# Spreading each output-projection tile over four slots, two tiles a unit, and writing the batches out instead of looping

## The chip, the cores and the metric

The kernel runs on one core of one Trainium2 chip. The metric is the device time of one execution in microseconds (us); lower is better. Engines are called as in the profile: PE (TensorE, with its weight loads as PEld), DVE (VectorE), ACT (ScalarE), POOL (GpSimd) and SP, which only issues DMAs here. DVE, ACT, POOL and PE each run their own instructions in order and wait for each other through semaphores.

## What is computed

One transformer layer on x of shape (8, 1024, 512): causal attention with 16 heads of 32, its output projection, a layer norm and a residual, then a feed-forward part of width 2048 with a sine inside, again with layer norm and residual.

```python
def _L0_attn_ref(h, Wqvk, Wo):
    b, s, d = h.shape
    qvk = (h @ Wqvk).reshape(b, s, 3, H, HD)
    q, v, k = (qvk[:, :, 0], qvk[:, :, 1], qvk[:, :, 2])
    scores = jnp.einsum('bshi,bthi->bsth', q, k) + mask[None, :, :, None]
    weights = jax.nn.softmax(scores / math.sqrt(d), axis=2)
    wv = jnp.einsum('bsth,bthi->bshi', weights, v).reshape(b, s, d)
    return wv @ Wo
...
x = x + _layernorm(_L0_attn_ref(_layernorm(x), Wqvk, Wo))
x = x + _layernorm(_L0_ffn_ref(_layernorm(x), W1, b1, phases, w_real, w_imag, W2, b2))
```

## The kernel before

There are three phases one after the other: the projections to q, v and k, the attention, and the feed-forward part. The change touches the attention alone. Attention works through 8 batches. A batch is 4 **units** of 4 heads each, and a unit is 20 **slots** (`NS`): a slot is one block of 256 queries against 128 keys for the four heads, in the order of `STEPS`. A loop over slots is written out in Python for every engine, and each engine's program goes through the same slots (`for u, k in stage.slots`), so that a slot number names the same step on all of them.

What stands in slot k of a unit:

- PE: the scores of slot k (`scores`, into `a_pst`, two banks, so it waits until ACT has taken slot k-2), in two parts of two heads; the weighing of V with the probabilities of the slot six earlier (`weigh`, `LAG` = 6, into `a_acc`), in two parts; and between them shared items: **pieces** (score blocks of the next unit into `a_pw`, from which DVE takes row maxima), the turning of a maximum, and the turning of attended rows. A piece goes into one of two banks, and waits until DVE has released the piece two before it.
- ACT: the exponential of slot k (`a_prob`), then the float16 high half of the slot before (`a_prob_hi`), which is done for two slots at a time where the table allows it.
- POOL: the low half, `a_prob_lo = a_prob - a_prob_hi`, which `weigh` waits for.
- DVE: maxima of the pieces (`u_mx`), normalising (`a_rden`, `a_o`), and copying the turned rows into `a_oT`.

The **output projection** takes the attended rows of a batch, held turned in `a_oT`, and multiplies them by Wo: 8 tiles of 128 rows a batch, each tile 4 groups (`g`) of 3 matmuls of 128x512 into one bank (`a_pwo`). A tile belongs to the batch before, and is fitted into the slots of the units that follow. `WO_AT` gives the slot at which each tile starts, counted from the start of the batch's fourth unit: 10, 18, ..., 66. That puts the tiles at slots 10 and 18 of the fourth unit, 6 and 14 of the next batch's first, 2, 10 and 18 of its second and 6 of its third. Groups 0 and 1 stand at the very end of the tile's first slot and 2 and 3 at the end of the second. DVE then takes the tile's row statistics (`wo_stats`) two slots after its start, a reciprocal square root in eight small steps, and writes the result (`wo_out`) six slots after, which frees the bank.

```python
WO_AT = list(range(10, 10 + 8 * QT, 8))
WO_STATS, WO_OUT, WO_STORE = 2, 6, 7
...
                    for part in range(2):
                        for b, t in stage.tiles(u, k, part):
                            for g in range(2 * part, 2 * part + 2):
                                project(i, before, b, t, g, stage, parity)
```

The first batch (`FIRST`), the last (`LAST`) and what is left after it (`DRAIN`) are written out; the six between them run as a hardware loop of three rounds with two batches a round (`run_all`), in which the counts that instructions wait for are worked out in registers. The tiles of the last batch have a table of their own, `WO_AT_LAST`.

Of the kernel before, what the change touches and what calls it, by code (L numbers as in the profile page):

```python
# [23 lines left out]
F16 = mybir.dt.float16  # L24
# [5 lines left out]
P = 128  # L30
BATCH, SEQ, D = 8, 1024, 512
# [12 lines left out]
GROUPS = HEADS // HPG  # L44
# [110 lines left out]

WO_AT = list(range(10, 10 + 8 * QT, 8))


WO_AT_LAST = [10, 15, 20, 21, 25, 26, 28, 29]
OWN_BANK = {3: 0, 4: 1, 5: 2, 6: 3}  # L160
WO_STATS, WO_OUT, WO_STORE = 2, 6, 7
LAST_OUT, LAST_STORE = 3, 4
ROOT_STEPS = 8
ROOT_AT = {(2, 1): (0,), (3, 0): (1,), (3, 1): (2,), (4, 0): (3,), (4, 1): (4,), (5, 0): (5,), (5, 1): (6,), (6, 0): (7,)}

ROOT_BITS, ROOT_NEAR, ROOT_GAIN = 0x5F1FFFF9, 2.38924456, 0.703952253

assert all(TURN_AT[t // TQ] < at < 2 * NS + TURN_AT[t // TQ] for t, at in enumerate(WO_AT))
TAIL = WO_AT_LAST[-1] + LAST_STORE + 1 - NS
# [894 lines left out]
def attention_phase(nc, x, weights, units, feed, qk_parts, v_parts, x1, b2):  # L1064
# [11 lines left out]
    with ctx:  # L1076
        def sb(name, shape, dt=F32):
            return ctx.enter_context(nc.sbuf_tensor("a_" + name, shape, dt))
# [15 lines left out]
        o = sb("o", [P, 2, TQ, P])  # L1094
        oT = sb("oT", [P, 2, GROUPS + 1, SEQ], F16)
        stats = sb("stats", [P, YR, 6])
# [44 lines left out]

        FIRST_ON_POOL = QT * (BATCH - 1) + min(t for t, at in enumerate(WO_AT_LAST) if at + WO_STATS >= NS)

# [18 lines left out]
        def turned_group(g, batch_parity):  # L1162
            return GROUPS if g == 0 and batch_parity else g

        def run_all(engine, run):

            run(0, FIRST, 0)
            with engine.Fori(0, BATCH // 2 - 1) as pair:
                run(2 * pair + 1, MIDDLE, 1)
                run(2 * pair + 2, MIDDLE, 0)  # L1170
            run(BATCH - 1, LAST, 1)
            run(BATCH, DRAIN, 0)

        def sync(sp):
# [41 lines left out]

            run_all(sp, run)

        def tensor(pe):
# [126 lines left out]
            run_all(pe, run)  # L1346

        def scalar(act):
# [37 lines left out]
            act.wait_ge(const, CONST)  # L1386
            run_all(act, run)

        def vector(dve):
# [76 lines left out]
            def roots(i, stage, u, k, late):  # L1466

                for (lag, end), steps in ROOT_AT.items():
                    for b, t in stage.tiles(u, k, lag):
                        if end == late and not stage.last_batch(b):  # L1470
                            for step in steps:
                                wo_root(i + b, t, step)

# [38 lines left out]

            run_all(dve, run)

        def gpsimd(pool):
# [18 lines left out]
            def run(i, stage, parity):  # L1534
                for u, k in stage.slots:
# [491 lines left out]
```

## Time and profile before

| what | us |
|---|---|
| median of the runs (range) | 3295.58 (3291.59 to 3298.58) |
| the profiled execution: its time, its span | 3292.4, 3290.4 |
| projections to q, v, k, up to about | 564 |
| attention: first and last exponential | 564.2 to 1896.3 |
| busy over the span: PE, DVE, ACT, POOL | 3143.2, 2316.0, 2062.5, 1284.6 |

The profile is of one execution. Busy time of PE counts overlapping matmuls and says little about how much room is left; the starts of its instructions say more. In the attention phase the start of an exponential on ACT marks the slot, so the distance between the first exponentials of two units is the length of a unit, and four of them make a batch.

### The profile page before, as it was taken

Reading aid. Unit: us, or ns where it says so; the run is one execution under the profiler, and the core shown is the slowest. Engines: PE = TensorE matmul, PEld = TensorE weight load, DVE = VectorE, ACT = ScalarE, POOL = GpSimd, SP = SyncE. Lnnn points to the kernel's source line nnn. Section 1 sums busy time; section 2 is a strip of 40 time slices with the busy share of each in tenths; the row PEclk is TensorE's granted clock in tenths of the full one; section 3 lists DMA queues with packets and bytes.
Section 4 is the critical chain, followed back from the end, with each engine's and each line's share of the span. In section 5 each row is a group of like instructions: output and inputs, shape, how many; then the busy total and the mean of one; then the engine's idle time right before and its main releaser. Section 6 shows DMA issues by size and latency. Waiting matters only on the chain.

```text
span 3290.4 us, 77730 instructions
## 1 busy us (share of the span) xinstructions
PE 3143.2 (96%) x30020; PEld 1825.9 (55%) x30020; DVE 2316.0 (70%) x4747; ACT 2062.5 (63%) x2453; POOL 1284.6 (39%) x586
## 2 busy tenths in 40 slices
PE   7999999999998999899999899999999999999998
PEld 3444444776666676666676644444444444444443
DVE  5655556888887888788888756666666666666665
ACT  2223333998988898889898944554555454545453
POOL 1000000998988898989898910000000000000000
PEclk9999999999999999999999999999999999999999
DMA  4564853122222222222222230000000000000000
GB/s 150 194 211 140 264 186 118 54 67 86 74 86 71 75 75 81 75 85 75 77 75 82 69 141 26 26 26 26 25 23 16 18 20 25 25 25 25 26 26 26
DMA packets 194241, 246.65 MB, mean 75 GB/s; under 512 B 16960, under 2 KB 135936, under 8 KB 191872
## 3 DMA queue, kind: packets, MB, share of 16 engines
q1 hardware_dynamic: 193920, 242.25, 23.5%
q8 instruction: 216, 3.54, 0.5%
q14 instruction: 105, 0.86, 0.1%
HBM read 148.87 MB, written 92.80 MB: 73 GB/s over the span
## 4 chain that ended last, share of the span: by engine, by line
PE 59%; POOL 24%; issue 11%; DVE 4%; ACT 1%; DMA 1%; POOLq 0%; SPq 0%; ACTq 0%; DVEq 0%
POOL a_prob_lo L1522 24%; PE f_py L1915 20%; PE f_ph L1892 20%; PE q_pm L903 14%; DVE u_mx L330 1%; PE f_ph L1877 1%; PE q_pt L893 1%; PE a_acc L1307 1%; ACT a_prob_hi L1363 1%; PE a_pwo L1260 1%; PE a_pst L1278 0%; PE a_pw L311 0%; DMA qk_parts<-q_stage 0%; DVE s_work L234 0%; DVE q_amax L792 0%
## 5 line engine op out<-in xcount | busy, mean ns | idle before, releaser
L1522 POOL TENSOR_TENSOR a_prob_lo<-a_prob,a_prob_hi 128x2048 f16<-128x2048 f32 (+2 forms) x448 | 1191.7, 2694 | 146.0 <-ACT a_prob_hi L1363 145.0
L330 DVE TENSOR_REDUCE u_mx<-a_pw 128x1 f32<-128x512 f32 x1184 | 731.7, 656 | 179.2 <-PE a_pw L316 116.7
L1353 ACT ACTIVATE a_prob<-a_pst,a_lift,w_exp_scale 128x1024 f32<-128x1024 f32 (+1 forms) x640 | 707.2, 1122 | 133.5 <-PE a_pst L1278 92.5
L1915 PE MATMUL f_py<-f_w,f_act 128*128 128x512 f16 x3048 | 699.4, 379 | 1.3 <-DMA f_w<-w_parts 1.3
L1363 ACT ACTIVATE a_prob_hi<-a_prob 128x2048 f16<-128x2048 f32 (+2 forms) x448 | 583.3, 1302 | 0.0
L1849 ACT ACTIVATE f_hidden_work<-f_ph,w_turn,w_fold 128x512 f32<-128x512 f32 x256 | 199.2, 778 | 598.3 <-PE f_ph L1892 597.7
L1307 PEld LDWEIGHTS a_acc<-u_vt,a_prob_hi 128*128 128x128 f16 x9216 | 422.7, 96 | 130.4 <-POOL a_prob_lo L1522 39.4
L1307 PE MATMUL a_acc<-u_vt,a_prob_hi 128*128 128x33 f16 x9216 | 448.6, 178 | 45.3 <-POOL a_prob_lo L1522 34.9
L1278 PE MATMUL a_pst<-u_qp,u_kp 98*128 98x256 f16 (+1 forms) x2560 | 462.0, 262 | 30.8 <-ACT a_prob L1353 14.9
L241 POOL TENSOR_TENSOR s_ve<-s_mv,s_eps 128x4 f32<-128x4 f32 x31 | 8.9, 286 | 1235.9 <-DVE s_mv L227 1235.9
L1915 PEld LDWEIGHTS f_py<-f_w,f_act 128*128 128x128 f16 x3048 | 297.7, 98 | 348.5 <-DVE f_act L1757 2.6
L311 PE MATMUL a_pw<-u_kp,u_qp 96*128 96x512 f16 x1494 | 440.0, 328 | 34.9 <-DVE u_mx L330 28.5
L1307 PE MATMUL a_acc<-u_vt,a_prob_lo 128*128 128x33 f16 x4608 | 426.3, 177 | 0.0
L1771 DVE TENSOR_SCALAR f_hidden_work<-f_hidden_work 128x512 f32<-128x512 f32 x256 | 108.2, 423 | 392.5 <-ACT f_hidden_work L1849 390.6
L1307 PEld LDWEIGHTS a_acc<-u_vt,a_prob_lo 128*128 128x128 f16 x4608 | 363.3, 96 | 0.0
L903 PE MATMUL q_pm<-q_xT,q_w 128*128 128x512 f16 x1536 | 344.2, 381 | 2.6 <-DVE q_w L817 2.6
L1892 PE MATMUL f_ph<-f_xT,f_w 128*128 128x512 f16 x1152 | 264.3, 379 | 0.0
L1892 PE MATMUL f_ph<-s_xT,f_w 128*128 128x512 f16 x1152 | 264.3, 379 | 0.0
L1278 PEld LDWEIGHTS a_pst<-u_qp,u_kp 98*128 98x128 f16 x2560 | 194.4, 97 | 116.8 <-ACT a_prob L1353 22.4
L903 PEld LDWEIGHTS q_pm<-q_xT,q_w 128*128 128x128 f16 x1536 | 150.4, 98 | 177.5 <-issue 6.4
L843 ACT ACTIVATE q_stage<-q_pm 128x512 f16<-128x512 f32 x128 | 76.3, 597 | 243.9 <-PE q_pm L903 215.7
L1757 DVE TENSOR_TENSOR f_act<-f_hidden_work,f_act 128x512 f16<-128x512 f32 x256 | 177.1, 692 | 39.3 <-ACT f_act L1839 39.3
(197 smaller groups left out, 4043.4 us busy)
## 6 DMA issues: line engine op xcount, KB each, us to landing
qk_parts<-q_stage SPq DMA_DIRECT2D x128, 256.0 KB, 3.4
u_qp<-qk_parts SPq DMA_DIRECT2D x192, 128.0 KB, 2.6
u_kp<-qk_parts SPq DMA_DIRECT2D x192, 128.0 KB, 2.7
v_parts<-q_vstage SPq DMA_DIRECT2D x16, 1056.0 KB, 5.3
u_vt<-v_parts SPq DMA_DIRECT2D x32, 528.0 KB, 4.5
q_x<-in_L_attn_h_dram SPq DMA_DIRECT2D x16, 1024.0 KB, 10.2
q_raw<-in_L_ffn_W_dram SPq DMA_DIRECT2D x16, 1024.0 KB, 8.0
u_xr<-in_L_attn_h_dram SPq DMA_DIRECT2D x64, 256.0 KB, 3.0
```

Of the source, the lines that this page charges most:

```text
L311: last = pe.matmul(out[:, s * n:(s + 1) * n], units.qp[b][0:KQ, i // TPC, h, i % TPC * P:(i % TPC + 1) * P], units.kp[b][0:KQ, h, half_ * ...
L330: dve.tensor_reduce(out, src[:, 0:n * len(heads)].rearrange("p (h n) -> p h n", n=n), AX_X, ALU.max).then_inc(units.released, 1)
L903: return pe.matmul(pm[:, m % BANKS, :], lhs, rhs, **flags)
L1278: last = pe.matmul(pst[:, slot, h, off:QC], kp[b][:, h, j * P:(j + 1) * P], qp[b][:, c * QC // CH, h, c * QC % CH + off:c * QC % CH + QC], ...
L1307: last = pe.matmul(acc[:, (t * HPG + h) * VF:(t * HPG + h + 1) * VF], part[:, k % HR, h, t * P:(t + 1) * P], vt[:, b, j, col:col + VF], st ...
L1353: act.activation(prob[:, k % PR, :, off:QC], pst[:, k % 2, :, off:QC], ACT.Exp, scale=exp_scale, bias=lift[:, :]).then_inc(exp_done, 1)
L1363: act.activation(prob_hi[:, first % HR:first % HR + steps, :, off:QC], prob[:, first % PR:first % PR + steps, :, off:QC], ACT.Copy).then_i ...
L1522: pool.tensor_tensor(prob_lo[:, first % HR:first % HR + steps, :, off:QC], prob[:, first % PR:first % PR + steps, :, off:QC], prob_hi[:, f ...
L1757: dve.tensor_tensor(act_r[:, r, 1, :], arg[:, s, :], act_r[:, r, 0, :], ALU.subtract).then_inc(act_lo, 1)
L1849: act.activation(arg[:, s, :], ph[:, bank_of("hidden", f), :], ACT.Identity, bias=turn0[:, f:f + 1], scale=fold[:, 0:1]).then_inc(arg_done, 1)
L1892: last = pe.matmul(ph[:, bank_of("hidden", f), :], w1_of(a, k, f), xT_of(e, b, k), start=(j == 0), stop=(j == len(terms) - 1))
L1915: last = pe.matmul(py[:, t, :], act_r[:, f % AR, b, t * P:(t + 1) * P], w2_of(a, f), start=(f == 0 and j == 0), stop=(f == NF - 1 and j == ...
```

## The change

A tile now starts every 10 slots instead of every 8 (`WO_AT`), so that every unit has two, at slots 0 and 10, in the same places. It runs over four slots instead of two, one group of 3 matmuls in each, and the group stands ahead of the slot's weighing instead of at the slot's end. DVE's statistics, steps and output move with it: four and eight slots after the tile's start instead of two and six. The last tiles of a batch are read while the next batch's second unit is being turned, so `a_oT` holds groups 0 and 1 twice instead of group 0 alone. The last batch's own tiles keep their two slots and their delays (`LAST_PARTS`, `LAST_STATS`), but stand ahead of the weighings too. The loop over batches is gone: all eight batches are written out, with constants in place of registers.

```diff
-WO_AT = list(range(10, 10 + 8 * QT, 8))
+WO_AT = list(range(10, 10 + 10 * QT, 10))
...
-WO_STATS, WO_OUT, WO_STORE = 2, 6, 7
-LAST_OUT, LAST_STORE = 3, 4
+WO_STATS, WO_OUT, WO_STORE = GROUPS, GROUPS + 4, GROUPS + 5
+LAST_PARTS, LAST_STATS, LAST_OUT, LAST_STORE = 2, 2, 3, 4
...
-        oT = sb("oT", [P, 2, GROUPS + 1, SEQ], F16)
+        oT = sb("oT", [P, 2, GROUPS + 2, SEQ], F16)
...
-            return GROUPS if g == 0 and batch_parity else g
+            return GROUPS + g if g < 2 and batch_parity else g
...
-            with engine.Fori(0, BATCH // 2 - 1) as pair:
-                run(2 * pair + 1, MIDDLE, 1)
-                run(2 * pair + 2, MIDDLE, 0)
+            for i in range(1, BATCH - 1):
+                run(i, MIDDLE, i % 2)
...
+            def tiles_of_slot(i, u, k, before, stage, parity):
+
+                for part in range(GROUPS):
+                    for b, t in stage.tiles(u, k, part):
+                        parts = LAST_PARTS if stage.last_batch(b) else GROUPS
+                        for g in range(part * GROUPS // parts, (part + 1) * GROUPS // parts if part < parts else 0):
+                            project(i, before, b, t, g, stage, parity)
...
                         if part >= 2 and e:
                             weigh(i, *e, part - 2)
+                        if part == 1 and e and stage.this:
+                            tiles_of_slot(i, u, k, before, stage, parity)
...
-                    for part in range(2):
-                        for b, t in stage.tiles(u, k, part):
-                            for g in range(2 * part, 2 * part + 2):
-                                project(i, before, b, t, g, stage, parity)
+                    if not (e and stage.this):
+                        tiles_of_slot(i, u, k, before, stage, parity)
```

How the instructions move, in three places. First PE, in the second unit of a middle batch of the kernel before, slot 2 and the start of slot 3. `a_pst` are scores, `a_pw` pieces, `a_acc` the weighing (it goes on for 24 matmuls), `a_pwo` the tile.

```order
L1278 MATMUL a_pst<-u_qp,u_kp 128x256 x2
L1061 REGISTER_ALU
L311 MATMUL a_pw<-u_kp,u_qp 128x512
L316 MATMUL a_pw<-u_mask_q,u_identb 128x128
L1296 REGISTER_ALU
L1307 MATMUL a_acc<-u_vt,a_prob_hi 128x33 x2
...
L1307 MATMUL a_acc<-u_vt,a_prob_lo 128x33
L1061 REGISTER_ALU
L1260 MATMUL a_pwo<-w_wo,a_oT 128x512 x6
L1061 REGISTER_ALU
L1278 MATMUL a_pst<-u_qp,u_kp 128x256 x2
```

The same slot 2 of a unit in the kernel after. Slots 0, 1 and 3, and 10 to 13, have the same shape:

```order
L1276 MATMUL a_pst<-u_qp,u_kp 128x256 x2
L1258 MATMUL a_pwo<-w_wo,a_oT 128x512 x3
L311 MATMUL a_pw<-u_kp,u_qp 128x512
L316 MATMUL a_pw<-u_mask_q,u_identb 128x128
L1305 MATMUL a_acc<-u_vt,a_prob_hi 128x33 x2
```

Six matmuls at the end of the slot became three between the slot's second scores and its weighing; the other three are in slots 0, 1 and 3.

Second, PE at the end of the loop's body in the kernel before, from the last turning of slot 19:

```order
L1241 MATMUL a_pw<-u_ident,a_o 128x128 x2
...
L1307 MATMUL a_acc<-u_vt,a_prob_lo 128x33
L1260 MATMUL a_pwo<-w_wo,a_oT 128x512 x6
L1168 REGISTER_ALU
L1168 COMPARE_AND_BRANCH
```

In the kernel after, PE has no branch anywhere in the attention phase; the next unit's scores follow.

Third, DVE in the kernel after, in slots 13 to 15 (`a_stats` are a tile's statistics, `a_root` the steps of its root, `u_mx` the maxima of pieces):

```order
L330 TENSOR_REDUCE u_mx<-a_pw 128x2
L1418 CAST a_oT<-a_pw 128x256
L1420 TENSOR_TENSOR a_oT<-a_pw,a_oT 128x256
L1426 BN_STATS a_stats<-a_pwo 128x6
L1428 COPY a_seen<-a_stats 128x1
L1429 BN_AGGR a_mv<-a_stats 128x2
L330 TENSOR_REDUCE u_mx<-a_pw 128x2
L330 TENSOR_REDUCE u_mx<-a_pw 128x1 x2
L1439 TENSOR_SCALAR a_root<-a_mv,w_wo_eps 128x1
L1443 TENSOR_SCALAR a_root<-a_root 128x1
L330 TENSOR_REDUCE u_mx<-a_pw 128x1 x2
```

In the kernel before, the statistics of a tile at slot 10 stood ahead of slot 12's maxima; now they stand ahead of slot 14's three.

## Rows read from the trace of the kernel before

**Rows 1.** Stretches: first batch's fourth unit; three units of the fourth, of the last.

```profile
core 0: us, PE busy (x) PEld busy (x) DVE busy (x) ACT busy (x) POOL busy (x), PEclk, DMA share, GB/s
675.65:716.09 40.44, 37.38 (x630) 28.21 (x628) 31.70 (x72) 37.45 (x36) 37.74 (x15) 1.00 0.23 67
1054.94:1181.94 127.00, 118.32 (x2007) 88.58 (x2006) 106.53 (x260) 112.75 (x102) 108.36 (x42) 1.00 0.28 80
1729.00:1856.60 127.60, 118.08 (x2007) 88.68 (x2006) 106.38 (x261) 112.86 (x102) 111.05 (x43) 1.00 0.30 89
```

**Rows 2.** Stretches: a unit without tiles, and one with three.

```profile
600.70:638.10 37.40, 34.17 (x636) 27.07 (x635) 29.92 (x59) 37.03 (x35) 37.16 (x15) 1.00 0.21 60
1097.82:1141.20 43.38, 40.41 (x640) 29.32 (x638) 34.10 (x85) 37.61 (x35) 37.69 (x15) 1.00 0.30 85
```

**Rows 3.** Stretches: the first and the last of the six middle batches.

```profile
716.10:884.20 168.10, 155.92 (x2633) 116.64 (x2632) 138.34 (x333) 150.40 (x136) 148.97 (x57) 1.00 0.27 78
1561.40:1729.00 167.60, 155.88 (x2635) 116.80 (x2633) 138.63 (x335) 150.25 (x136) 148.98 (x57) 1.00 0.28 79
```

**Rows 4.** Waits, 714 to 1856 us: who waited for whom, total, times, longest.

```profile
ACT a_prob L1353 <- PE a_pst L1278: 88.1, 102, 1.6
ACT a_prob L1353 <- PE a_pst L1283: 37.0, 52, 3.4
```

**Rows 5.** ACT in time, unit without tiles: slots 0, 3, 4, 13 with 14.

```profile
600.77 1.22 ACT L1353 ACTIVATE a_prob<-a_pst,a_lift,w_exp_scale 128x1024 f32<-128x1024 f32 x1
...
605.60 1.23 ACT L1353 ACTIVATE a_prob<-a_pst,a_lift,w_exp_scale 128x1024 f32<-128x1024 f32 x1
607.07 1.21 ACT L1353 ACTIVATE a_prob<-a_pst,a_lift,w_exp_scale 128x1024 f32<-128x1024 f32 x1 [0.23 <-PE a_pst L1283]
...
624.37 2.57 ACT L1353 ACTIVATE a_prob<-a_pst,a_lift,w_exp_scale 128x1024 f32<-128x1024 f32 x2
```

**Rows 6.** ACT in time, unit 1097.82: exponentials of slots 4, 9 with 10, 14.

```profile
1106.59 1.21 ACT L1353 ACTIVATE a_prob<-a_pst,a_lift,w_exp_scale 128x1024 f32<-128x1024 f32 x1 [1.80 <-PE a_pst L1283]
...
1116.69 2.31 ACT L1353 ACTIVATE a_prob<-a_pst,a_lift,w_exp_scale 128x1024 f32<-128x1024 f32 x2
...
1128.12 1.20 ACT L1353 ACTIVATE a_prob<-a_pst,a_lift,w_exp_scale 128x1024 f32<-128x1024 f32 x1 [0.39 <-PE a_pst L1278]
```

**Rows 7.** PE in time: first scores of slots 0 and 4, unit 1054.94.

```profile
1053.85 0.39 PE L1278 MATMUL a_pst<-u_qp,u_kp 98*128 98x256 f16 x2 [2.62 <-issue]
...
1060.38 0.38 PE L1278 MATMUL a_pst<-u_qp,u_kp 98*128 98x256 f16 x2
```

**Rows 8.** PE in time, unit without tiles: slots 0, 10, a weighing, slot 14.

```profile
597.96 0.38 PE L1278 MATMUL a_pst<-u_qp,u_kp 98*128 98x256 f16 x2
...
616.70 0.38 PE L1278 MATMUL a_pst<-u_qp,u_kp 98*128 98x256 f16 x2
...
621.62 0.20 PE L1307 MATMUL a_acc<-u_vt,a_prob_hi 128*128 128x33 f16 x2 [0.27 <-POOL a_prob_lo L1522]
...
624.71 0.38 PE L1278 MATMUL a_pst<-u_qp,u_kp 98*128 98x256 f16 x2
```

**Rows 9.** PE in time, unit 1097.82: half a tile, slot 10, a piece, slot 14.

```profile
1104.09 1.46 PE L1260 MATMUL a_pwo<-w_wo,a_oT 128*128 128x512 f16 x6
...
1116.44 0.38 PE L1278 MATMUL a_pst<-u_qp,u_kp 98*128 98x256 f16 x2
...
1124.56 0.39 PE L311 MATMUL a_pw<-u_kp,u_qp 96*128 96x512 f16 x1 [0.47 <-DVE u_mx L330]
...
1127.15 0.38 PE L1278 MATMUL a_pst<-u_qp,u_kp 98*128 98x256 f16 x2
```

**Rows 10.** The loop's line on PE's sequencer; ACT behind and without the branch.

```profile
L1168 PEldq COMPARE_BRANCH  x3: 83/3959/4078, 1049.6 to 1726.4; - x3
1393.54 1.20 ACT L1353 ACTIVATE a_prob<-a_pst,a_lift,w_exp_scale 128x1024 f32<-128x1024 f32 x1 [3.38 <-PE a_pst L1283]
1222.63 1.20 ACT L1353 ACTIVATE a_prob<-a_pst,a_lift,w_exp_scale 128x1024 f32<-128x1024 f32 x1 [0.49 <-PE a_pst L1283]
```

More of the change, by code:

```diff
@@ L150 @@
 K_FREE_AT = max(k for k, (_c, j) in enumerate(STEPS) if j < TPC) + 1
-WO_AT = list(range(10, 10 + 8 * QT, 8))
+WO_AT = list(range(10, 10 + 10 * QT, 10))
 WO_AT_LAST = [10, 15, 20, 21, 25, 26, 28, 29]
 OWN_BANK = {3: 0, 4: 1, 5: 2, 6: 3}
-WO_STATS, WO_OUT, WO_STORE = 2, 6, 7
-LAST_OUT, LAST_STORE = 3, 4
+WO_STATS, WO_OUT, WO_STORE = GROUPS, GROUPS + 4, GROUPS + 5
+LAST_PARTS, LAST_STATS, LAST_OUT, LAST_STORE = 2, 2, 3, 4
 ROOT_STEPS = 8
-ROOT_AT = {(2, 1): (0,), (3, 0): (1,), (3, 1): (2,), (4, 0): (3,), (4, 1): (4,), (5, 0): (5,), (5, 1): (6,), (6, 0): (7,)}
+ROOT_AT = {(WO_STATS + (n + 1) // 2, (n + 1) % 2): n for n in range(ROOT_STEPS)}
 ROOT_BITS, ROOT_NEAR, ROOT_GAIN = 0x5F1FFFF9, 2.38924456, 0.703952253
-assert all(TURN_AT[t // TQ] < at < 2 * NS + TURN_AT[t // TQ] for t, at in enumerate(WO_AT))
+assert all(TURN_AT[t // TQ] < at < 3 * NS + TURN_AT[t // TQ] for t, at in enumerate(WO_AT))
 TAIL = WO_AT_LAST[-1] + LAST_STORE + 1 - NS
@@ L1139, in attention_phase @@
         BANKS_LEFT = 6
-        FIRST_ON_POOL = QT * (BATCH - 1) + min(t for t, at in enumerate(WO_AT_LAST) if at + WO_STATS >= NS)
+        FIRST_ON_POOL = QT * (BATCH - 1) + min(t for t, at in enumerate(WO_AT_LAST) if at + LAST_STATS >= NS)
         def on_pool(n):
@@ L1162, in turned_group, with run_all @@
         def turned_group(g, batch_parity):
-            return GROUPS if g == 0 and batch_parity else g
-        def run_all(engine, run):
+            return GROUPS + g if g < 2 and batch_parity else g
+        def run_all(run):
             run(0, FIRST, 0)
-            with engine.Fori(0, BATCH // 2 - 1) as pair:
-                run(2 * pair + 1, MIDDLE, 1)
-                run(2 * pair + 2, MIDDLE, 0)
+            for i in range(1, BATCH - 1):
+                run(i, MIDDLE, i % 2)
             run(BATCH - 1, LAST, 1)
@@ L1215, in run @@
                             store_max(sp, units, unit % 2, half)
-            run_all(sp, run)
+            run_all(run)
         def tensor(pe):
@@ L1340, in run @@
                         last.then_inc(feed.tr_done, 1)
-                    for part in range(2):
-                        for b, t in stage.tiles(u, k, part):
-                            for g in range(2 * part, 2 * part + 2):
-                                project(i, before, b, t, g, stage, parity)
-            run_all(pe, run)
+                    if not (e and stage.this):
+                        tiles_of_slot(i, u, k, before, stage, parity)
+            run_all(run)
         def scalar(act):
@@ L1386, in scalar @@
             act.wait_ge(const, CONST)
-            run_all(act, run)
+            run_all(run)
         def vector(dve):
@@ L1466, in roots @@
             def roots(i, stage, u, k, late):
-                for (lag, end), steps in ROOT_AT.items():
+                for (lag, end), step in ROOT_AT.items():
                     for b, t in stage.tiles(u, k, lag):
                         if end == late and not stage.last_batch(b):
-                            for step in steps:
-                                wo_root(i + b, t, step)
+                            wo_root(i + b, t, step)
             def shared(i, at, before, what, unit, m, stage, parity):
@@ L1484, in run @@
                     for b, t in stage.tiles(u, k, WO_STATS):
+                        if not stage.last_batch(b):
+                            wo_stats(i + b, t, stage)
+                    for b, t in stage.tiles(u, k, LAST_STATS):
+                        if not stage.last_batch(b):
+                            continue
                         wo_stats(i + b, t, stage)
-                        if stage.last_batch(b) and stage is not DRAIN:
+                        if stage is not DRAIN:
                             for step in range(ROOT_STEPS):
@@ L1511, in run @@
                         scale_rows(dve, feed, 0, 1, feed.work, feed.xin[:, 0], feed.normed)
-            run_all(dve, run)
+            run_all(run)
         def gpsimd(pool):
@@ L1540, in run @@
                         deviations(pool, feed, 0, 1)
-                    for b, t in stage.tiles(u, k, WO_STATS):
+                    for b, t in stage.tiles(u, k, LAST_STATS):
                         if stage is DRAIN:
@@ L1552, in gpsimd @@
             pool.wait_ge(units.v_stored, 16 * NCH + START)
-            run_all(pool, run)
+            run_all(run)
         turned_last = (released, work_before(BATCH, DRAIN) + len(DRAIN.work))
```

## The prediction

> **What bounds the kernel now.** The change acts in the attention alone, 1332 us of the profiled execution's 3292.4. I first cut the trace into stretches that end at the first exponential of a unit, and compared units with and without tiles. The first batch's second unit has none and lasts 37.40 us, a unit with three lasts 43.38 [rows 2]; the busy columns, in the order of the heading in [rows 1], give ACT 37.0 and 37.6, POOL 37.2 and 37.7. So ACT and POOL are full in the unit without tiles, and what the tiles add, ACT spends idle. The waits say for whom: ACT waited for scores 88.1 + 37.0 us between 714 and 1856 [rows 4]. The six middle batches take 1729.0 - 716.1 = 1012.9 us [rows 3], 42.2 a unit.
>
> A tile is 12 matmuls of 128x512. Six of them take 1.46 us with the last one's own tail of about 0.38, so one starts every 0.215 [rows 9], a group of three costs PE 0.65 and a tile 2.58. The question is how much of it PE can take without making ACT late.
>
> Two quantities settle it. The first is ACT's pace with nothing to wait for: in slots 0 to 3 the exponentials start 4.83 us apart from slot 0 to slot 3 and the fourth needs 1.09 (605.60 to 607.07 is 1.47, of which 0.38 is late scores) [rows 5]: 5.92. In slots 10 to 13 it is 7.2: slot 13's exponential and the next take 2.57 together [rows 5] where two at full pace take 2.31 [rows 6], so that unit loses 0.27 there. ACT's floor for a unit is 37.40 - 0.38 - 0.27 = 36.8. The second is PE's lead: the time from the first score of a slot to its exponential. It is 600.77 - 597.96 = 2.81 at slot 0 [rows 5, 8] and about 1.0 to 1.2 when ACT only just has to wait (at slot 4 the scores follow the tile at 1104.09 + 6 x 0.215 = 1105.38, and 1106.59 - 1105.38 = 1.21; at slot 14 1128.12 - 1127.15 = 0.97) [rows 6, 9].
>
> **The tile at slots 0 to 3.** Without a tile PE needs 1060.38 - 1053.85 = 6.53 us for these four slots when nothing holds it [rows 7]. With four groups it is 6.53 + 2.58 = 9.11. It starts 2.81 ahead, so slot 4's scores begin 6.30 after slot 0's exponential, and slot 4's exponential follows at 6.30 + 1.21 = 7.51, against the floor of 5.92: **1.6 us** late. Today's tile at slots 2 and 3 makes the same exponential 1106.59 - 1097.82 = 8.77 after the start [rows 2, 6], 2.9 late: there PE first idles in slots 0 to 2 for the low halves and then works the whole tile in a row. The new groups stand ahead of the weighing, where that wait is, and fill it. Bounds: 1.2, should the lead at slot 0 grow by 0.4, and 2.9.
>
> **The tile at slots 10 to 13.** The unit without tiles goes from slot 10 to slot 14 in 624.71 - 616.70 = 8.01 on PE [rows 8]. Adding up the starts that are further apart than such matmuls otherwise are, 1.15 of it are waits: 0.45 for a low half in front of slot 12's weighing (the row shows 0.27 of it as idle), the rest small ones for the banks of the pieces. That leaves 6.86, with a tile 9.44. Unit 1097.82, whose tile starts at slot 10 in the old way, needs 1127.15 - 1116.44 = 10.71 [rows 9]. I take 9.6: the low half is there 0.65 later for nothing, and DVE, which in these slots has nine maxima at some 0.63, a normalising, a turning and a maximum to split, about 8 us when no statistics fall into them, keeps up with a PE that needs 9.4. The lead at slot 10 is 1116.69 + 1.09 - 1116.44 = 1.34 [rows 6, 9]. Slot 14's exponential is then at -1.34 + 9.6 + 1.0 = 9.3 after slot 10's, **2.1 us** over 7.2. Bounds: 1.9 (no waits left) and 1128.12 - 1117.78 - 7.2 = 3.1, what the tile costs now.
>
> **What moves on DVE** I cost at nothing. Statistics at slot 4 fall where PE has 1.9 us of work and ACT 2.9. At slot 14 they delay three maxima by about 1 us; ACT's slot is again 2.9 long, and PE has 3.3 us of work in slots 14 and 15 against 4.0 of ACT, so with a lead of 1.0 it can lose about 0.7 to 1 before ACT sees it. If that cover is gone it costs up to 0.5 a unit. DVE's present wait for a tile, as its statistics come right behind it, ends: two slots lie between now. The bank is free two slots after `wo_out` as before. The first tile of a batch, at slot 10 of the fourth unit, now comes sooner after the turning of slot 9 that it needs: 0 to 0.5 in one unit of four. The second copy of group 1 in `a_oT` adds no instruction.
>
> **A unit** thus takes 36.8 + 1.6 + 2.1 = 40.5 us. POOL needs 37.7 [rows 2], 2.8 less. Six batches: 24 x 40.5 = 972.0.
>
> **The loop.** PE's branch takes 3959 and 4078 ns the two times it is taken, 83 the third [rows 10]; behind a taken one ACT idles 3.38 us for scores, at the same place without a branch 0.49 [rows 10], so a jump costs 2.9 and two 5.8. The Trainium skill bears on this: "Runtime: NRT & Kernel Launch", Instruction fetch mechanics, says that a taken branch whose target is not in the fetched window stops execution until it is fetched, and the trace agrees with its 3.96 and 4.08 us. "Advanced Engine Details and Errata", Control Flow Timing, gives about 108 ns for a compare-and-branch; the sum by that would be an estimate of 0.2 us in place of 5.8, and the row decides against it. The register instructions that vanish cost nothing now: the last batch, written out with constants already, is no faster in its first three units than the fourth, 127.60 and 127.00 us [rows 1].
>
> **The sum**, against the profiled 3292.4:
> - two jumps: -5.8
> - the other units of the six middle batches: 972.0 - (1012.9 - 5.8) = -35.1
> - the last batch's first three units, 127.6 now [rows 1], 121.5 then: -6.1
> - the first batch's fourth unit has one tile instead of two, 40.4 [rows 1] to 36.8 + 0.4 + 2.1 = 39.3: -1.1
> - the last batch's fourth unit gets a tile at slot 0 that it did not have; at most 1.6, but POOL bounds that unit: +1.0
>
> Together -47.1, so 3245.3 for the profiled execution; it lies 3.2 under the median of 3295.58, so the median becomes **3248**. A measurement here tells about 0.2% (6.6 us) from no change.
>
> **The rivals.**
> 1. *DVE's waits remain* (0.14). The piece at 1124.56 waited 0.47 for DVE [rows 9], right behind a tile's statistics. If the pieces of slots 12 to 15 go on waiting, because DVE carries two tiles in each unit where it now has one to three, the second tile keeps its 3.1 and slot 14 adds 0.5: 36.8 + 1.6 + 3.1 + 0.5 = 42.0 a unit. 27 units (24 + 3) are then 1134 against 1140.5 with their jumps, and the kernel ends at about 3289. Half of it gives 41.25 and 3269. For it: DVE is busy 34.1 us of 43.4 with three tiles and 29.9 of 37.4 with none [rows 2], and not evenly. Against: the statistics left the crowded slot 12.
> 2. *Spreading does nothing, two tiles a unit cost their full price* (0.07), the case on the slower side. PE has no wait left in slots 0 to 3 of unit 1053.85 [rows 7], and a PE that is late stays late, in four slots as in two. Then each unit pays 2.9 + 3.1: 42.8, 27 units 1155.6, that is 15 more than now: about 3311. It decides from 42.24 a unit on. Against: the lead of 2.81 at slot 0, which today's tiles at slots 2, 6 and 10 hardly use.
> 3. *More is hidden* (0.09): the lead at slot 0 grows, slots 10 to 13 lose all waits, and the following slots carry some of it: 39.7 a unit or less, 3226 or below.
> 4. *The written-out program pays in fetching what the jumps cost* (0.04). The last batch is written out already, and its first three units take 127.60 where the fourth batch's take 127.00 [rows 1]: 0.6 a batch, six times 3.6 of the 5.8, 3252, inside the range.
>
> **How the numbers follow.** The forecast, 39.9 to 41.5 a unit, has 0.66, and rival 4 lies within it with 0.04. Its own bounds (27 x 0.6 = 16 down, 27 x 1.0 = 27 up) give 3232 to 3275; the range reaches a little into rivals 1 and 3: **3228 to 3276**. Faster by over 0.2%: 0.66 + 0.04 + 0.09 and 0.11 of rival 1; within 0.2%: 0.04, the far end of rival 1 and the near end of 2; slower: 0.06.
>
> **What the profile will show.** Units all alike near 40.5 us, and batches near 162. PE's first scores of slot 4 some 6.3 after slot 0's exponential. No wait for a low half in front of the weighings of slots 0, 2 and 12. ACT's wait for scores in attention down from 125 to about 100 us. No idle of 3 us at 1051 and 1389. I am wrong if units differ by place as now, if pieces wait for DVE in slots 14 and 15 with ACT idle behind them, or if slot 0's lead is well below 2.8.

## The result, and the profile after

| kernel | median us (range, executions) | ratio to before | 95% interval |
|---|---|---|---|
| before | 3295.01 (3291.59 to 3298.58, 4) | | |
| after | 3254.27 (3253.64 to 3255.36, 4) | 0.9877 | 0.9859 to 0.9894 |

The median falls by 40.7 us; the forecast was 3248, 6 us too low. The profiled execution of the kernel after took 3255.4 us, with a span of 3253.6, where the sum said 3245.3: 10 too low. The difference is that the forecast added 3.2 for the distance of a profiled execution from the median, and this one lies 1.1 above its own. Attention, from first to last exponential, went from 1332.1 to 1295.6 us (563.2 to 1858.8).

First the stretches of the kernel after: a unit of the first middle batch, that whole batch, three units of the third middle batch and of the last batch, and the last unit. They answer to [rows 1 to 3].

```profile
core 0: us, PE busy (x) PEld busy (x) DVE busy (x) ACT busy (x) POOL busy (x), PEclk, DMA share, GB/s
714.69:755.29 40.60, 38.24 (x659) 29.38 (x658) 35.10 (x83) 37.27 (x35) 37.17 (x15) 1.00 0.31 82
714.69:877.46 162.77, 153.26 (x2634) 117.58 (x2633) 140.40 (x332) 149.12 (x137) 148.70 (x57) 1.00 0.30 82
1040.42:1162.20 121.78, 114.36 (x1971) 87.85 (x1970) 105.24 (x249) 111.53 (x103) 111.09 (x43) 1.00 0.28 80
1692.14:1813.94 121.80, 114.75 (x1975) 88.14 (x1974) 105.29 (x249) 111.84 (x103) 111.49 (x43) 1.00 0.25 73
...
1813.94:1858.79 44.85, 32.51 (x544) 24.36 (x543) 31.68 (x72) 36.15 (x33) 41.80 (x17) 0.84 0.24 80
```

Units no longer differ by place: 40.6 us for the first three of each batch, 40.9 for the fourth, and a batch 162.8 instead of 168.1 and 167.6. ACT and POOL are busy as long as before; what went is ACT's idle time. Only the last unit is worse, 44.85 against 39.7 before.

Next the waits from 714 to 1856 us: who waited for whom, total us, times, longest. They answer to [rows 4].

```profile
PEld a_acc L1305 <- POOL a_prob_lo L1532: 45.8, 84, 1.1
...
ACT a_prob L1359 <- PE a_pst L1276: 41.8, 64, 1.5
ACT a_prob L1359 <- PE a_pst L1281: 32.3, 29, 1.4
...
PEld a_pw L311 <- DVE u_mx L330: 28.4, 56, 0.7
...
PE a_pw L311 <- DVE u_mx L330: 15.1, 28, 0.6
```

ACT's wait for scores is 74.1 us; it was 125.1 [rows 4]. A further 19.8 us of such waits (19 times) is booked as for POOL. In the unit below that happens at slot 14, 1.03 us behind PE's first scores of that slot (1108.49), which is the lead that the forecast gave an exponential that only just waits for scores. So I count them as scores too: 93.9, near the forecast's 100. What came last there, POOL or PE, the runs don't take apart.

Now ACT in time, unit 1081.38, exponentials of slots 0, 3, 4, 13 and 14 (answers to [rows 6]):

```profile
1081.38 1.22 ACT L1359 ACTIVATE a_prob<-a_pst,a_lift,w_exp_scale 128x1024 f32<-128x1024 f32 x1
...
1086.58 1.21 ACT L1359 ACTIVATE a_prob<-a_pst,a_lift,w_exp_scale 128x1024 f32<-128x1024 f32 x1 [0.23 <-PE a_pst L1276]
1088.93 1.20 ACT L1359 ACTIVATE a_prob<-a_pst,a_lift,w_exp_scale 128x1024 f32<-128x1024 f32 x1 [1.15 <-PE a_pst L1281]
...
1107.28 1.21 ACT L1359 ACTIVATE a_prob<-a_pst,a_lift,w_exp_scale 128x1024 f32<-128x1024 f32 x1 [0.91 <-PE a_pst L1276]
1109.52 1.20 ACT L1359 ACTIVATE a_prob<-a_pst,a_lift,w_exp_scale 128x1024 f32<-128x1024 f32 x1 [1.03 <-POOL a_prob_lo L1532]
```

And PE there: the first scores of slots 0, 4 and 10, and the first group of the tile (answers to [rows 7, 9]):

```profile
1078.57 0.38 PE L1276 MATMUL a_pst<-u_qp,u_kp 98*128 98x256 f16 x2
...
1079.45 0.81 PE L1258 MATMUL a_pwo<-w_wo,a_oT 128*128 128x512 f16 x3
...
1087.68 0.38 PE L1276 MATMUL a_pst<-u_qp,u_kp 98*128 98x256 f16 x2
...
1098.68 0.38 PE L1276 MATMUL a_pst<-u_qp,u_kp 98*128 98x256 f16 x2
```

PE is 1081.38 - 1078.57 = 2.81 ahead at slot 0, needs 1087.68 - 1078.57 = 9.11 for the four slots and brings slot 4's scores 6.30 after slot 0's exponential: the three numbers of the forecast to the hundredth. Slot 4's exponential is 7.55 behind slot 0's, 1.63 over the 5.92 of ACT's pace. In slots 10 to 13 PE takes 1108.49 - 1098.68 = 9.81, a little more than the 9.6 of the forecast, with a lead of 1.44 instead of 1.34 and 1.03 left at slot 14: slot 14's exponential comes 9.40 behind slot 10's, 2.2 over the pace of 7.2. In this unit PE waits for low halves at slots 8 and 18 only, in front of none of the weighings of slots 0, 2 and 12.

### The profile page after: what moved, and what is told of

Read it like the earlier page. It is cut to its first block, busy times and chain, and to the rows that moved or that the text cites. A ratio compares the mean times of both kernels' runs of the same rounds, so it can differ in the third digit from the quotient of the medians.

```text
span 3253.6 us, 72496 instructions
## 1 busy us (share of the span) xinstructions
PE 3124.1 (96%) x30020; PEld 1831.8 (56%) x30020; DVE 2331.3 (72%) x4747; ACT 2054.9 (63%) x2453; POOL 1283.4 (39%) x586
## 4 chain that ended last, share of the span: by engine, by line
PE 80%; DVE 9%; POOL 5%; ACT 3%; issue 2%; DMA 1%; SPq 0%; ACTq 0%; POOLq 0%
PE f_py L1925 20%; PE f_ph L1902 20%; PE q_pm L903 15%; PE a_acc L1305 6%; PE a_pst L1276 5%; PE a_pw L311 5%; POOL a_prob_lo L1532 4%; PE a_pwo L1258 4%; DVE u_mx L330 4%; ACT a_prob_hi L1369 2%; PE a_pst L1281 1%; ACT a_prob L1359 1%; PE a_pw L316 1%; PE f_ph L1887 1%; PE q_pt L893 1%
## 5 line engine op out<-in xcount | busy, mean ns | idle before, releaser
L330 DVE TENSOR_REDUCE u_mx<-a_pw 128x1 f32<-128x512 f32 x1184 | 745.3, 657 | 143.4 <-PE a_pw L316 83.7
L1276 PE MATMUL a_pst<-u_qp,u_kp 98*128 98x256 f16 (+1 forms) x2560 | 461.8, 262 | 30.2 <-ACT a_prob L1359 27.5
L1305 PE MATMUL a_acc<-u_vt,a_prob_hi 128*128 128x33 f16 x9216 | 448.1, 178 | 40.5 <-POOL a_prob_lo L1532 27.9
L1276 PEld LDWEIGHTS a_pst<-u_qp,u_kp 98*128 98x128 f16 x2560 | 187.2, 97 | 90.0 <-ACT a_prob L1359 35.7
```

The lines of the kernel that those rows point to most:

```text
L330: dve.tensor_reduce(out, src[:, 0:n * len(heads)].rearrange("p (h n) -> p h n", n=n), AX_X, ALU.max).then_inc(units.released, 1)
L1276: last = pe.matmul(pst[:, slot, h, off:QC], kp[b][:, h, j * P:(j + 1) * P], qp[b][:, c * QC // CH, h, c * QC % CH + off:c * QC % CH + QC], ...
L1305: last = pe.matmul(acc[:, (t * HPG + h) * VF:(t * HPG + h + 1) * VF], part[:, k % HR, h, t * P:(t + 1) * P], vt[:, b, j, col:col + VF], st ...
```

## The experiments

Their ratios are to the kernel before, on the same chip; its medians there were 3293.2 to 3293.7. "A unit" is the distance of the first exponentials of two units.

**The loop kept.** The kernel after, with the hardware loop and its registers put back.

```diff
-            for i in range(1, BATCH - 1):
-                run(i, MIDDLE, i % 2)
+            with engine.Fori(0, BATCH // 2 - 1) as pair:
+                run(2 * pair + 1, MIDDLE, 1)
+                run(2 * pair + 2, MIDDLE, 0)
```

> The kernel after with the six middle batches in the hardware loop again, all else as it is there. My theory: the two taken branches give back 2.9 us each and nothing else changes, 3254.3 + 5.8 = 3260; every unit stays 40.6 to 40.9 apart from the two behind a jump. Rival, the register instructions of the loop cost time too, now that TensorE is late in more slots: units longer by 0.1 or more everywhere, 3265 or above. Rival, the jump costs only its instruction, 0.1 us each: 3254.5.

3269.87 us, ratio 0.993 (0.9913 to 0.9946): 15.6 over the kernel after, more than twice what was expected. Its branch on PE, PE's first scores behind it and ACT's waits:

```profile
L1168 PEldq COMPARE_BRANCH  x3: 82/4613/4739, 1037.2 to 1705.5; - x3
...
1042.11 0.60 PE L1278 MATMUL a_pst<-u_qp,u_kp 98*128 98x256 f16 x2 [4.42 <-issue]
1043.79 1.48 PE L1260 MATMUL a_pwo<-w_wo,a_oT 128*128 128x512 f16 x3
...
1044.04 1.20 ACT L1361 ACTIVATE a_prob<-a_pst,a_lift,w_exp_scale 128x1024 f32<-128x1024 f32 x1 [3.56 <-PE a_pst L1283]
...
1047.81 0.78 ACT L1361 ACTIVATE a_prob<-a_pst,a_lift,w_exp_scale 128x512 f32<-128x512 f32 x1 [2.06 <-PE a_pst L1283]
```

The stretches before and behind the branch (columns as above), and behind that of the kernel before:

```profile
1028.00:1037.50 9.50, 8.41 (x175) 6.68 (x174) 9.19 (x25) 9.50 (x8) 7.03 (x3) 1.00 0.16 47
1037.50:1042.10 4.60, 0.19 (x8) 0.08 (x4) 0.62 (x2) 2.98 (x3) 4.60 (x2) 0.92 0.41 126
1042.10:1045.50 3.40, 3.39 (x14) 1.74 (x14) 0.69 (x1) 1.46 (x2) 3.08 (x2) 0.50 0.54 159
1045.50:1049.00 3.50, 3.50 (x48) 2.55 (x47) 1.38 (x2) 1.44 (x3) 1.16 (x1) 0.62 0.30 80
```

```profile
1050.90:1053.80 2.90, 0.33 (x2) 0.00 (x0) 0.23 (x1) 0.78 (x1) 2.90 (x1) 1.00 0.64 170
1053.80:1057.00 3.20, 3.15 (x63) 2.62 (x64) 3.00 (x9) 2.06 (x3) 2.85 (x3) 1.00 0.34 86
```

The jump takes 0.65 longer, and then three things come together. PE's lead at slot 0, which the new tile uses up, is gone. The granted clock is 0.50, the lower level (1.2 GHz), for 3.4 us, and 0.62 in the next 3.5; before, it stayed at 1.00. The tile's three matmuls take 1.48 instead of 0.81. The unit that ends with the jump takes 44.7 (44.8 at the second) and the one behind it 44.2 (44.3), in place of 40.9 and 40.6: 7.5 a jump by these rounded lengths, 14.4 for two against the very same units of the kernel after. A jump costs 2.9 us in the old order and over 7 in the new one. How that divides among the three, no run takes apart.

The other twenty units of the middle batches are together 3.3 us longer than in the kernel after, and the last batch's first three 1.1. In nearly all the longer ones PE waits for a small transfer (4 KB, into `u_qp`); the waits from 714 to 1856 us, here and in the kernel after:

```profile
PE a_pst L1278 <- DMA u_qp<-u_nm: 10.0, 14, 1.2
```

```profile
PE a_pst L1276 <- DMA u_qp<-u_nm: 1.8, 4, 0.7
```

Away from the jumps, middle units without such a wait are 40.6 to 40.7 long, as in the kernel after, so the registers, which stand in all of them, cost under 0.1 a unit. Only the third unit in each round is 40.9 without it, which stays open. The time alone, 3269.87, would not have told this from the rival on registers, which said 3265 or above. Attention is 18.0 us longer in this trace than in that of the kernel after, while the whole execution is 13.2 longer: the part behind attention is 4.4 shorter (1390.4 against 1394.8), and what makes it so is open.

**Written out alone.** The kernel before, with only that part of the diff (the one above, turned round).

> The kernel before with its batches written out and nothing else changed. My theory: two jumps of 2.9 us go, 3295 - 5.8 = 3289, and the written-out batches run as the fourth did, 42.9, 43.4, 40.7 and 40.9 us a unit. Rival, straight code pays in fetching: 0.6 a batch back, 3292 to 3293. Rival, the register instructions cost time: under 3285.

3289.14 us (10 executions), ratio 0.9989 (0.998 to 0.9999). The jumps are gone, and 4 of the expected 5.8 us show. Its units run as the loop's do or 0.05 to 0.1 shorter (42.80, 43.39 and 40.69 against 42.92, 43.40 and 40.74), so straight code costs nothing that shows here. Two places in its trace give some back: one unit of the fifth batch is 2.6 longer than its like, where PE waited for a small DMA, and the last unit takes 43.7 instead of 39.7. Both come up again below.

**Even places alone.** All of the kernel after but the four slots and the place ahead of the weighing.

```diff
-WO_STATS, WO_OUT, WO_STORE = GROUPS, GROUPS + 4, GROUPS + 5
+WO_STATS, WO_OUT, WO_STORE = 2, 6, 7
...
-                        parts = LAST_PARTS if stage.last_batch(b) else GROUPS
+                        parts = LAST_PARTS
...
-                        if part == 1 and e and stage.this:
-                            tiles_of_slot(i, u, k, before, stage, parity)
...
-                    if not (e and stage.this):
-                        tiles_of_slot(i, u, k, before, stage, parity)
+                    tiles_of_slot(i, u, k, before, stage, parity)
```

> The kernel after, but each tile again in two slots, its six matmuls at the end of each slot, and statistics and output two and six slots after the start as before. So this is the even placing alone, tiles at slots 0 and 10 of every unit. My theory: spreading and the place ahead of the weighing carry the gain; a tile at slots 0 and 1 costs 2.1 us and one at 10 and 11 its old 3.1: 36.8 + 2.1 + 3.1 = 42.0 a unit, 27 x 1.35 = 36 us more than after, about 3290. Rival, the even placing is what gains: within 5 us of 3254.

3291.43 us, ratio 0.9993 (0.9983 to 1.0002): nothing. Units take 41.9, the mean of the uneven ones. Two tiles a unit are worth nothing by themselves. Some units of its trace are longer, up to 44.2; in that one PE waits 1.73 us for the small transfer.

**Four slots, at the slot's end.** The kernel after with only the last two pieces of that diff.

> The kernel after with each tile over four slots, but its group of three matmuls at the end of the slot, behind the weighing. My theory: TensorE waits 0.5 us for the low half in slot 0 again, which the group no longer fills, and slot 4's exponential is that much later; in slot 12 the low half is there by then. 41.1 us a unit, 27 x 0.5 = 13 us more: 3268. Rival, only the number of slots matters: 3254, no wait for a low half in slot 0 or as many as are hidden elsewhere. Rival, both waits come back in full (slot 0 and slot 12): 3280.

3272.09 us, ratio 0.9935 (0.9919 to 0.9952), 41.3 a unit. Spreading brings 19 us over the last kernel and the place ahead of the weighing a further 18. Of the 19, the shorter units are 27 x 0.54 = 14.6; most of the rest are the single long units of the last kernel, which this trace doesn't have (PE waits 0.4 us for the small transfer, there 9.9). Why the place matters, from PE in time, the first weighing of a slot 0:

```profile
1085.49 0.22 PE L1305 MATMUL a_acc<-u_vt,a_prob_hi 128*128 128x33 f16 x2 [0.34 <-POOL a_prob_lo L1529]
```

PE stands idle for the low half and then does the group; in the kernel after the group fills that wait. PE waits 35.9 us (82 times) for low halves in this kernel and 21.8 (57) in the kernel after, once more a unit. Slot 4's exponential comes 8.08 behind slot 0's instead of 7.55: the 0.5 that was expected. The other 0.2 of the unit's 0.7 fall in slots 10 to 13 (9.60 instead of 9.40), where this trace shows no such wait; what they are is open.

**Later starts.** The kernel after with the tiles at slots 2 and 12 of a unit, and at 1 and 11. Shown is the first.

```diff
-WO_AT = list(range(10, 10 + 10 * QT, 10))
+WO_AT = list(range(12, 12 + 10 * QT, 10))
```

> The kernel after with every tile two slots later, at slots 2 to 5 and 12 to 15 of each unit; statistics and output move with it to slots 6 and 10, 16 and 20. My theory: what a tile costs is set by how much of TensorE's work falls into slots where ScalarE is slow (4 and 14 last 2.9 us for 1.9 and 1.8 us of matmuls), so the first tile costs 1.1 instead of 1.6 and the second 1.9 instead of 2.2: 39.8 a unit, 27 x 0.8 = 22 less, 3232. Rival, VectorE decides: its statistics now fall ahead of slots 6 to 10, which have two runs of three maxima, and pieces wait for it there; no gain, 3254 or more.

> The kernel after with every tile one slot later, at slots 1 to 4 and 11 to 14. By the same theory half of that gain: 40.2 a unit, 3243. By the rival about 3254, since statistics at slots 5 and 15 are as good as at 4 and 14.

3281.76 us (ratio 0.9965, 0.9951 to 0.9979) and 3281.96 (0.9964, 0.995 to 0.9978), 41.8 a unit both: the rival. At slots 2 to 5 PE's part went as hoped, 1.1 over ACT's pace in place of 1.6. But pieces wait for DVE, in the first of them:

```profile
PEld a_pw L311 <- DVE u_mx L330: 67.4, 162, 0.6
...
PE a_pw L311 <- DVE u_mx L330: 27.5, 81, 0.5
```

162 and 81 waits instead of 56 and 28, behind statistics and steps that now stand among the maxima of slots 6 to 10. In the unit at 1089.16 PE waits so at slots 7, 8 and 10, and what the unit loses there (slot 10's exponential 12.6 behind slot 4's instead of 11.2) is more than the 0.5 gained before.

**Statistics twice.** The kernel after with each tile's first statistics done twice, the first into a spare tile: 0.6 us more for DVE a tile, with nothing else changed.

```diff
+                dve.bn_stats(again[:, :], projected(t, stage))
                 dve.bn_stats(a_stats[:, :], projected(t, stage))
```

> The kernel after with each tile's row statistics (0.69 us) taken twice by VectorE, the first time into a tile that nobody reads. Slot 4 has room. At slot 14 a piece already waits 0.70 us for VectorE, and TensorE's lead at slot 16 is 1.04 us, as small as it gets, so ScalarE is only just not held up. My theory: the second statistics show up nearly in full there, 0.6 a unit, 27 x 0.6 = 16 more: 3270. Rival, VectorE has room to spare, as its share of busy time (about 85%) suggests: within 4 us of 3254.

3282.7 us, ratio 0.9966 (0.9952 to 0.998): 41.6 a unit, so 1.2 us of work on an engine that is busy 35 of 40.6 cost 1.0 us of time, where 0.6 was expected. PE in time, the third piece of slot 14, here and in the kernel after:

```profile
1119.87 0.39 PE L311 MATMUL a_pw<-u_kp,u_qp 96*128 96x512 f16 x1 [1.14 <-DVE u_mx L330]
```

```profile
1110.49 0.39 PE L311 MATMUL a_pw<-u_kp,u_qp 96*128 96x512 f16 x1 [0.55 <-DVE u_mx L330]
```

The kernel after waits 0.55 for DVE at this slot, and ACT's long slot hides it: slot 16's exponential comes 3.99 behind slot 14's, as in the kernel before. With 0.59 more of waiting it comes 4.51 behind: 0.5 of the 1.0, so there is no reserve. The other 0.45 are lost before slot 14 (28.59 into the unit instead of 28.14), where "slot 4 has room" was expected: a piece waits 0.42 for DVE 15.6 us into the unit, which in the kernel after none does.

**Roots on POOL.** In the kernel after, the eight steps of each root are taken from DVE and done by POOL in two instructions. DVE's busy time in a batch falls from 140.4 to 132.3 us by it, POOL's rises from 148.7 to 154.2.

```diff
-                            for step in range(ROOT_STEPS):
-                                wo_root(i + b, t, step)
...
+                    for b, t in stage.tiles(u, k, WO_STATS):
+                        if not stage.last_batch(b):
+                            last_tile_root(t, QT * (i + b) + t)
```

> The kernel after, with the eight-step root of every tile of the middle batches taken off DVE: POOL makes it in two instructions (add, power), as the last tiles have it already. DVE is freed of 8 small instructions a tile, some 1.5 us, and POOL gets about 0.75 us a tile. Theory (DVE stands exactly at its edge, PE is the bound at 40.6 us a unit): as PE's order is unchanged, little comes back; 40.2 to 40.6 a unit, 3244 to 3255 us. Rival (POOL, at 38 us of 40.6, makes low halves late when it gets 1.5 us more a unit): 41.0 a unit or more, 3265 us.

> The same roots on POOL, and the tiles at slots 2 and 12 of each unit. With the roots on DVE these places gave 41.8 us a unit, and the traces put it down to DVE, whose statistics delayed pieces, while PE at slots 2 to 5 lost only 1.1 in place of 1.6. Theory (that was DVE): with 3 us a unit fewer on DVE the waits for pieces shrink, and the unit goes to 39.8 to 40.6, 3232 to 3255 us. Rival A (it is the two statistics themselves, behind which three maxima queue, not the roots): 41.5 or more, 3274 us and above. Rival B (POOL is late instead): waits for low halves appear, 41.2 or more.

> The same roots on POOL, with the tiles at slots 1 and 11 of each unit. With roots on DVE these places gave 41.8 us a unit. Theory (DVE was the cause): 40.1 to 40.6 a unit, 3240 to 3255 us. Rival A (statistics, not roots): 41.5 or more, 3274 us and above. Rival B (POOL late): waits for low halves appear, 41.2 or more.

At the old places 3250.09 us (3249.26 to 3252.16), ratio 0.9872 (0.9855 to 0.9888), units 40.5: DVE's relief returns 0.1 a unit, and by the intervals the kernel is not told from the kernel after. Its second middle batch, for the load (POOL is the last column of busy time):

```profile
875.93:1038.42 162.49, 152.77 (x2634) 117.73 (x2633) 132.25 (x268) 149.31 (x137) 154.21 (x73) 1.00 0.28 81
```

At slots 2 and 12, 3264.01 us (0.9917, 0.99 to 0.9933), 41.1 a unit instead of 41.8; at 1 and 11, 3276.4 (0.9952, 0.9936 to 0.9969), 41.5 instead of 41.8. The waits of the first:

```profile
PEld a_pw L311 <- DVE u_mx L330: 39.4, 108, 0.5
...
PE a_pw L311 <- DVE u_mx L330: 6.8, 27, 0.3
```

The waits for DVE fell from 27.5 to 6.8 us on PE and the time with them, 17.8 us, so DVE was a cause of the loss at those places. It was not all of it: 41.1 lies between theory and both rivals, and 41.5 is where rival A began. The traces show rival B's sign as well, POOL late. PE in time at slot 0's weighing, in the first kernel and in the second:

```profile
1122.92 0.22 PE L1305 MATMUL a_acc<-u_vt,a_prob_hi 128*128 128x33 f16 x2 [0.61 <-POOL a_prob_lo L1527]
```

```profile
1128.65 0.21 PE L1305 MATMUL a_acc<-u_vt,a_prob_hi 128*128 128x33 f16 x2 [0.77 <-POOL a_prob_lo L1527]
```

With the roots on DVE this wait is 0.29 at either place, and no group of a tile stands in front of it at slots 1 or 2. Slot 4's exponential now comes 7.22 instead of 7.03 behind slot 0's in the first kernel, and 7.85 instead of 7.36 in the second. An estimate from this: POOL takes back 0.2 and 0.5 a unit, and DVE's relief by itself is worth 0.9 and 0.7. In all, PE waits 17.4 and 21.5 us for low halves instead of 7.7 and 7.9. What keeps the rest, with the roots gone from DVE, stays open.

**The last unit.** The scaling of the first rows of the feed-forward part (`scale_rows`, 4 instructions) moved from slot 14 to 17 of the last unit, behind the normalising.

```diff
-    FEED_LOAD, FEED_STATS, FEED_SCALE = 0, 6, 14
+    FEED_LOAD, FEED_STATS, FEED_SCALE = 0, 6, 17
```

> The kernel after with the four scalings of the feed-forward part's first rows moved in VectorE's order from the end of slot 14 of the very last unit to the end of slot 17, behind the normalising that TensorE waits for. In the kernel after they take 10.75 us beside GpSimd and TensorE then waits 8.4 us for that normalising; the last unit is 44.8 us. My theory: that wait goes, the last unit is near 39 us, and some of it comes back since the scaled rows are later: 3249. Rival, the rows are needed as soon as the last unit ends, so all of it comes back: 3254, or later.

3256.26 us, ratio 0.9885 (0.9869 to 0.9902), not faster. PE in time at the end of attention, in the kernel after and in this one:

```profile
1856.57 0.22 PE L1305 MATMUL a_acc<-u_vt,a_prob_hi 128*128 128x33 f16 x2 [8.39 <-DVE a_o L1411]
```

```profile
1850.68 0.20 PE L1305 MATMUL a_acc<-u_vt,a_prob_hi 128*128 128x33 f16 x2 [1.71 <-DVE a_o L1411]
...
1862.61 1.86 PE L1258 MATMUL a_pwo<-w_wo,a_oT 128*128 128x512 f16 x4 [8.70 <-DVE a_oT L1420]
```

The last unit shrinks from 44.8 to 37.9, and a wait as long stands one step later. The scaling itself takes long. Its line in the last unit of the kernel before, of the kernel written out alone, of the kernel after, with one of the feed-forward part and POOL's line beside it (ns, shortest, median, longest):

```profile
L234 DVE TENSOR_SCALAR s_work<-s_x,s_mv,s_rstd x4: 1372/1949/4303, 1881.1 to 1886.2; 128x512 f32<-128x512 f32 x4
```

```profile
L234 DVE TENSOR_SCALAR s_work<-s_x,s_mv,s_rstd x4: 1377/2994/4298, 1876.1 to 1883.3; 128x512 f32<-128x512 f32 x4
```

```profile
L234 DVE TENSOR_SCALAR s_work<-s_x,s_mv,s_rstd x4: 1024/2829/4308, 1842.2 to 1848.7; 128x512 f32<-128x512 f32 x4
...
L234 DVE TENSOR_SCALAR s_work<-s_x,s_mv,s_rstd x4: 540/543/544, 2016.3 to 2017.7; 128x512 f32<-128x512 f32 x4
...
L1532 POOL TENSOR_TENSOR a_prob_lo<-a_prob,a_prob_hi x4: 1346/4242/4265, 1842.9 to 1852.7; 128x2048 f16<-128x2048 f32 x3, 128x512 f16<-128x512 f32 x1
```

## Why the forecast came close, and where its sum was off

**The mechanism holds.** The four slots, and the group ahead of the weighing, did what the sum said: 9.11 us of PE with no wait, 1.63 late at slot 4 (forecast 1.6), 2.2 at slots 10 to 13 (2.1, where 0.2 more on PE and 0.1 more lead partly cancel). Rival 2 (spreading does nothing) is refuted by the ladder: written out 3289, even places 3291, four slots 3272, ahead of the weighing 3254. Taken in this order, nearly the whole gain is from these last two steps. Rival 3 did not come: slot 0's lead stayed 2.81. Rival 4, pay in fetching, is tested by the kernel written out alone, whose units are no longer than the loop's; in the kernel after all batches are straight code, so their equal lengths say nothing on it.

**Term by term.** The profile shows -36.5 in attention for the -47.1 of the sum.
- *Six batches and two jumps*, forecast 972.0: 1692.14 - 714.69 = 977.4, 5.4 more. A unit is 40.6 instead of 40.5, the fourth 40.9 (a wait for the turning of slot 9, forecast 0 to 0.5, is 0.3), and two or three units are 0.2 to 0.4 over their like.
- *The last batch's first three units*: 121.8, forecast 121.5.
- *The first batch's fourth unit*: 39.2, as forecast. But the batch ends 0.7 later than the sum has it, as its first unit, which the change doesn't touch, is 37.5 instead of 36.5.
- *The last unit*: forecast +1.0, measured +5.1. This term was off by 4.1 us, two fifths of the whole miss, and the one whose mechanism was wrong; the six batches are off by more in sum, but by half a per cent of their 972.

**The step that failed** is "at most 1.6, but POOL bounds that unit: +1.0". I looked at what the tile costs PE and at POOL's busy time, and not at DVE's scaling there. Up to slot 18 the unit is hardly longer than before (its exponential comes 35.0 us after slot 0's, before 34.7); what is new stands in front of slot 19's, 9.8 behind it instead of 5.0. ACT's wait there, before and after:

```profile
1896.29 0.78 ACT L1353 ACTIVATE a_prob<-a_pst,a_lift,w_exp_scale 128x512 f32<-128x512 f32 x1 [2.01 <-PE a_pst L1283]
```

```profile
1858.79 0.78 ACT L1359 ACTIVATE a_prob<-a_pst,a_lift,w_exp_scale 128x512 f32<-128x512 f32 x1 [6.83 <-PE a_pst L1281]
```

PE waits in front of it for DVE's `a_o`, 3.6 us before and 8.4 after. In DVE's order the scaling stands ahead of `a_o` and ends 3.0 before it in both. The scaling takes 9.34 us in the kernel before (from 1881.13 on) and 10.75 after (from 1842.23), where its like take 0.54 each. Each of the four ends about 0.3 behind one subtraction of POOL: that from 1844.23 takes 4.27, and the scaling from 1844.47 takes 4.31. Before, one of the four sat out the whole of a 128x2048 subtraction, after, two did.

The larger part is that DVE comes to the scaling later, 28.3 us into the unit instead of 24.5. So of the 5.1 us, 3.8 are the later start and 1.4 the longer scaling, to rounding. The kernel written out alone has the old places, and yet two long ones (4.30 and 4.28), a start at 26.5 and a last unit of 43.7: a unit 4.0 longer comes about without the new tile. How much of the later start in the kernel after is the tile's, no run takes apart. With roots on POOL three of the four fell where POOL had no subtraction and took 0.54 each, and yet the last unit is 43.3 long: there DVE waits 4.4 for a root that stands behind POOL's subtractions. So DVE and POOL hold that unit between them in either kernel, and the scaling alone is not all of it.

The Trainium skill has the rule that fits the long scalings: "SBUF — State Buffer", Who interferes with whom, says that a DVE instruction in a two-port mode contends with GpSimd, and that whichever issues first holds the shared ports for its whole instruction while the other is blocked. The trace agrees with the exclusion: 4.3 us, until POOL is through, and not some share more; whether this scaling runs in such a mode no row shows. The experiment on its place shows that moving it by three slots is no cure: PE then waits 8.70 for the next thing, `a_oT`.

**DVE's moves "at nothing"** is right in its sum and was luckier than it read. The forecast allowed a loss of 0.7 to 1 us at slot 14 before ACT would see it. PE waits 0.55 there, and 0.6 us more of DVE a tile, in "statistics twice", cost 1.0 a unit, half of it at slot 14. The cover is about used up. So what rival 1 feared, pieces that wait for DVE, is the state of the kernels with later starts (41.8 a unit, near the 42.0 that it was given, though at slots 7 to 10 and not only at 12 to 15), and not of this one.

**The loop, "a jump costs 2.9"**, is the right size for the order of before and the wrong one for the order after. Written out alone brought 4, and written out in the new order 15.6, not all of it at the jumps. A sum over parts can't show that, as the price depends on the lead that the other part uses.

**Left open**: what but POOL's low halves keeps the later starts at 41.1 and 41.5 with DVE relieved; and the single long units. One of them, in the kernel written out alone, has this wait on PE, and then the clock:

```profile
1227.15 0.56 PE L1276 MATMUL a_pst<-u_qp,u_kp 98*128 98x256 f16 x2 [1.50 <-DMA u_qp<-u_nm]
...
1224.30:1227.20 2.90, 1.40 (x31) 1.16 (x28) 2.40 (x6) 2.90 (x4) 1.75 (x3) 1.00 0.31 102
1227.20:1229.50 2.30, 2.30 (x32) 1.75 (x33) 1.03 (x2) 1.87 (x3) 2.30 (x1) 0.51 0.95 248
```

PE waits 1.50 us for a transfer of 4 KB and then runs for 2.3 us at a granted clock of 0.51; the unit is 2.6 longer. An estimate from these two rows, 1.5 and half of 2.3, comes to that. Why the transfer is late in single units wasn't tried; PE's waits for it from 714 to 1856 us are 6.7 us in the kernel before, 9.9 with the even places alone and 0.4 with the four slots at the slot's end.

## What to carry to other kernels

Where an engine works ahead of the one that bounds the time, count its lead at each place, and put extra work where the lead is largest, in small groups just ahead of the instructions that would otherwise wait; moving the same work about without splitting it brought nothing here. A lead can be spent only once: when one change uses it, look again at every stall that it covered, because a jump that cost 2.9 us cost over 7 afterwards. And before costing work on a third engine at nothing, add a little of it in an experiment and see whether the time moves.

## What the runs showed of the hardware that was not expected

- A DVE scaling of 128x512 in float32 from SBUF to SBUF took 0.54 us alone and 4.3 us when it met POOL's 128x2048 subtraction, ending 0.3 behind it; with shorter subtractions (1.35 us for 128x512, 2.31 for 128x1024) it took 1.37 and 2.35.
- TensorE's granted clock fell to half behind an idle of 4.42 us in one kernel and behind a wait of 1.50 us in another, and stayed at full behind the 2.62 us idle of the kernel before [rows 7]. The length of the idle time alone doesn't decide it.
- The same taken branch took 3.96 and 4.08 us in one kernel and 4.61 and 4.74 in another on PE, and 40 to 63 ns on each of the other engines.
